# Indirect scatters and gathers issued one at a time in a fused attention and mixture-of-experts layer

## The reference

```python
x = x + _layernorm(attn(_layernorm(x)))          # 16 heads, exp decay on the scores
# feed-forward part, flat = _layernorm(x) as 4096 x 256
out = einsum('tnm,nmd->td', silu(gs) * us, wd_s)             # 2 shared experts, 128 wide
probs = softmax(flat @ router_w)                             # 16 experts
weights, indices = top_k(probs, 2); weights /= weights.sum()
h = silu(g) * u * comb[:, :, None]                           # 16 routed experts, 64 wide
out = out + einsum('tem,emd->td', h, wd_r)
x = x + _layernorm(out)
```

## Time and profile before

| | us |
|---|---|
| three runs | 1548.79 to 1557.74, median 1553.58 |
| profiled execution | 1557.02 |
| its span | 1554.5 |
| attention and what is ahead of it | about the first 1119 |
| routing and blocks 0 to 3 of pairs, up to the first gather | 1119 to 1372 |
| pairs of the second sequence, with gathers of blocks 0 to 3 | 1372 to 1484 |
| gathers of blocks 4 to 7 and the end | 1484 to 1554 |

### The profile page before, as it was taken

The page is one execution under the profiler, slowest core; times in us unless marked ns, Lnnn a source line. Parts: engine busy times, 40 slices in busy tenths (PEclk is TensorE's granted clock), DMA queues, the critical chain, the costliest instruction groups (busy, mean ns, idle before and its releaser), DMA issues. The chain is left out here.

```text
span 1554.5 us, 27193 instructions
## 1 busy us (share of the span) xinstructions
PE 1342.6 (86%) x8496; PEld 603.5 (39%) x8497; DVE 553.2 (36%) x1704; ACT 1146.8 (74%) x1419; POOL 189.7 (12%) x239
## 2 busy tenths in 40 slices
PE   7759999999999999999999999999688766666681
PEld 4523333333333333333333333333356555545441
DVE  5603323233232232322313121122254754615634
ACT  4449999999999989999999999999544434313422
POOL 1000000000000000000000000000034522232363
PEclk9979999999999999999999999999888888888886
DMA  7575466555664557555665465459422433445532
GB/s 186 224 163 136 116 141 157 121 135 127 152 157 97 135 145 155 145 115 130 157 132 135 104 134 102 88 131 248 103 81 95 139 106 116 148 124 170 184 111 86
DMA packets 139538, 210.96 MB, mean 136 GB/s; under 512 B 56336, under 2 KB 102288, under 8 KB 130960
## 3 DMA queue, kind: packets, MB, share of 16 engines
q1 hardware_dynamic: 133328, 193.38, 50.3%
q0 software_dynamic: 6144, 16.79, 3.3%
HBM read 147.19 MB, written 67.11 MB: 138 GB/s over the span
## 5 line engine op out<-in xcount | busy, mean ns | idle before, releaser
L705 ACT ACTIVATE work<-ps 128x1024 f32<-128x1024 f32 x1024 | 951.4, 1084 | 71.9 <-DVE ps L541 38.0
L636 PE MATMUL ps<-work 128*32 128x512 f32 x4096 | 548.1, 607 | 0.0
L628 PE MATMUL ps<-Q_st,K_st 64*128 64x512 f32 (+3 forms) x2432 | 441.1, 430 | 44.6 <-ACT work L705 28.1
L628 PEld LDWEIGHTS ps<-Q_st,K_st 64*128 64x128 f32 x2432 | 231.3, 185 | 543.2 <-ACT work L705 452.0
L541 DVE TENSOR_TENSOR ps<-ps,small 128x128 f32<-128x128 f32 x512 | 153.3, 299 | 743.1 <-PE ps L628 741.5
L505 POOL COPY work<-V_all 128x256 f32 (+1 forms) x32 | 12.9, 403 | 924.3 <-PE ps L636 924.2
L636 PEld LDWEIGHTS ps<-work 128*32 128x32 f32 x4096 | 80.9, 108 | 114.0 <-issue 88.1
L2058 POOL DMA_INDIRECT xT<-y_dram,decay x64 | 64.1, 1002 | 60.8 <-DMA y_dram<-work 42.5
L2046 POOL DMA_INDIRECT xs_dram<-part,decay x64 | 64.0, 1000 | 47.5 <-issue 47.5
L2215 PE MATMUL ps<-stack,work 128*128 x384 | 61.0, 310 | 10.0 <-issue 9.8
L2197 PE MATMUL ps<-ident,work 128*128 128x128 f32 x192 | 35.9, 318 | 32.1 <-DVE work L2271 17.3
(11 more groups left out here) (181 smaller groups left out, 1035.8 us busy)
## 6 DMA issues: line engine op xcount, KB each, us to landing
K_st<-halves_dram SPq DMA_DIRECT2D x256, 256.0 KB, 5.6
halves_dram<-work SPq DMA_DIRECT2D x64, 512.0 KB, 3.7
Q_st<-halves_dram SPq DMA_DIRECT2D x256, 128.0 KB, 5.6
work<-xs_dram SPq DMA_DIRECT2D x96, 128.0 KB
y_dram<-work SPq DMA_DIRECT2D x48, 256.0 KB
work<-in_L_attn_x SPq DMA_DIRECT2D x16, 512.0 KB, 7.4
attn_dram<-work SPq DMA_DIRECT2D x16, 256.0 KB, 6.6
work<-attn_dram SPq DMA_DIRECT2D x8, 512.0 KB
```

Source lines behind the costliest of these rows:

```text
L628: m = nc.tensor.matmul(ps[:, half_of(s, half) + c % 2, q0 % CH:q0 % CH + w], K_st[tile, par, a, s * P:(s + 1) * P], Q_st[tile, par, a, at: ...
L636: m = nc.tensor.matmul(ps[STRIP * c:STRIP * (c + 1), ACC + par], Vg[:, par, s], probs[:, probs_of(par, s), chunk(c)], start=s == 0, stop=s ...
L705: nc.scalar.activation(probs[:, probs_of(par, s), half * HALF:(half + 1) * HALF], src, ACT.Exp, scale=SCALE).then_inc(s_["exp_done"], 1)
```

## The change

Three things are changed.

1. `few_calls` puts a wait ahead of each scatter, and ahead of each gather of blocks 0 to 3: it is issued when the one before it has landed. The gathers of blocks 4 to 7 get no such wait.
2. The places in `ORDER` move. The last four scatter calls of most blocks stand behind `S1` of the block after the next; `GA` becomes eight calls in four entries, and the additions `SM` of blocks 0 to 3 start at the slots 6, 10, 14 and 18, where they started at 5, 9, 13 and 16.
3. The loads of the attention result and of x for block 1 (`next_block`) are issued ahead of the store of the last pair of heads, inside the attention part.

```diff
@@ attention, SyncE
             first_block["weights"](sp, 1)
+            first_block["next_block"](sp)
             store_att(NPAIR - 1)
-            first_block["next_block"](sp)
@@ layer, ORDER
     for r in (1, 2):
         ORDER += [("T1", r + 1), ("LA", r + 2), ("D", r - 1, 0), ("Y", r + 1), ("Z", r - 1, 0), ("T2", r), ("D", r - 1, 1), ("S1", r + 1),
...
-        ORDER += [("SC", r, j) for j in range(CT)]
+                  ("SC", r - 1, 2), ("SC", r - 1, 3), ("LG", r), ("Z", r - 1, 1), ("N1", r + 1, 0), ("N1", r + 1, 1), ("LX", r + 2), ("U", r, 0), ("EX", r), ("U", r, 1), ("S2", r + 1),
+                  ("TP", r, 0), ("TP", r, 1), ("H", r, 0), ("RK", r), ("H", r, 1), ("N2", r + 1), ("PL", r), ("CA", r), ("SC", r, 0), ("SC", r, 1)]
...
-    behind[-1] += [("GA", 0), ("GA", 1)]
-    for n, i in enumerate((5, 9, 13, 16)):
+    behind[NP + 2] = []
+    for n, i in enumerate((6, 10, 14, 18)):
+        for j in range(CT):
+            behind[4 * n + j - 1].append(("GA", n, j))
         for k in range(4):
             behind[i + k].append(("SM", n, k))
         behind[i + 4] += [("ST", n, 0)]
         behind[i + 5] += [("ST", n, 1), ("F3", n)]
-        if n < 2:
-            behind[i + 5].append(("GA", n + 2))
@@ layer, GpSimd
+            def few_calls(done, k):
+                k -= 1
+                if k >= 0:
+                    n = k // (2 * CT)
+                    pool.wait_ge(done[n % 2], 16 * (2 * CT * (n // 2) + k % (2 * CT) + 1))
+
             def scatter(r, j):
...
                 for i in range(2):
+                    few_calls(put_done, 2 * CT * r + 2 * j + i)
                     at = put_at[:, r * CT + j, i:i + 1]
...
-            def gather(n):
+            def gather(n, j):
...
-                need(pool, sum_sb, 2 * (n - 1))
-                for j in range(CT):
-                    for i in range(2):
-                        at = get_at[:, n * CT + j, i:i + 1]
+                if j == 0:
+                    need(pool, sum_sb, 2 * (n - 1))
+                for i in range(2):
+                    if n < 4:
+                        few_calls(yg_in, 2 * CT * n + 2 * j + i)
+                    at = get_at[:, n * CT + j, i:i + 1]
```

More of the change, by code:

```diff
@@ L1572, in layer @@
         ORDER += [("P", 1, i)] + behind[i]
+    gathers = lambda n: [("GA", n, j) for j in range(CT)]
     sums = lambda n: [("SM", n, k) for k in range(4)]
@@ L1575, in layer @@
     norm = lambda n: [("N3", n, 0), ("N3", n, 1)]
-    ORDER += [("GA", 4), ("GA", 5), ("U", 5, 0), ("H", 5, 0), ("U", 5, 1), ("H", 5, 1), ("U", 6, 0), ("D", 5, 0), ("D", 5, 1), ("Z", 5, 0), ("Z", 5, 1), ("U", 6, 1)]
-    ORDER += sums(4) + [("H", 6, 0)] + stats(4) + [("F3", 4), ("GA", 6), ("U", 7, 0), ("H", 6, 1), ("D", 6, 0)] + norm(4) + [("D", 6, 1), ("Z", 6, 0), ("Z", 6, 1), ("U", 7, 1)]
-    ORDER += sums(5) + [("H", 7, 0), ("AD", 4)] + stats(5) + [("F3", 5), ("GA", 7), ("H", 7, 1), ("D", 7, 0), ("D", 7, 1)] + norm(5) + [("Z", 7, 0), ("Z", 7, 1)]
+    ORDER += gathers(4) + gathers(5) + [("U", 5, 0), ("H", 5, 0)] + behind[NP + 2] + [("U", 5, 1), ("H", 5, 1), ("U", 6, 0), ("D", 5, 0), ("D", 5, 1), ("Z", 5, 0), ("Z", 5, 1), ("U", 6, 1)]
+    ORDER += sums(4) + [("H", 6, 0)] + stats(4) + [("F3", 4)] + gathers(6) + [("U", 7, 0), ("H", 6, 1), ("D", 6, 0)] + norm(4) + [("D", 6, 1), ("Z", 6, 0), ("Z", 6, 1), ("U", 7, 1)]
+    ORDER += sums(5) + [("H", 7, 0), ("AD", 4)] + stats(5) + [("F3", 5)] + gathers(7) + [("H", 7, 1), ("D", 7, 0), ("D", 7, 1)] + norm(5) + [("Z", 7, 0), ("Z", 7, 1)]
     ORDER += sums(6) + [("AD", 5)] + stats(6) + [("F3", 6)] + norm(6)
@@ L2044, in scatter @@
                 for i in range(2):
+                    few_calls(put_done, 2 * CT * r + 2 * j + i)
                     at = put_at[:, r * CT + j, i:i + 1]
                     nc.gpsimd.indirect_dma_start(xs_dram[r // 4], bass.IndirectOffsetOnAxis(ap=at, axis=0), xn[r % 2][:, j], None).then_inc(put_done[r % 2], 16)
-            def gather(n):
+            def gather(n, j):
                 b = n // 4
-                if n % 4 == 0:
+                if n % 4 == 0 and j == 0:
                     pool.wait_ge(get_sb, b + 1)
@@ L2074, in _ @@
                 elif what == "GA":
-                    gather(n)
+                    gather(n, at[0])
                 elif what == "F3":
```

19 lines of the change are left out of this document (7 added, 12 removed).

## The result

The changed kernel takes 1579.2 us (median of four runs, 1579.1 to 1582.3). The kernel before, on the same chip, took 1555.7. The ratio is 1.0158, with an interval of 1.0112 to 1.0203: slower by some 24 us. The forecast was 1566, so the direction held and the time lies in the range, but half of the loss was not foreseen.

What follows compares the result with a forecast made beforehand. ScalarE's exps fill the unchanged attention part; in the last 440 us engines stall behind GpSimd's DMA trains. Routing +11 (start included), scatters -10, gathers +11.2: +12 on 1557.0, 1569, as median 1566 us; range 1535 to 1592.

Steps and rivals of the forecast that it cites:

- the standstills: After attention: VectorE and ScalarE idle with input ready while GpSimd's indirect calls run; some 54.5 us on the chain.
- remote: Profile's mark for idle time released by another core or an unknown queue; 11.0% of 495 us from 1060 on.
- the twelve: Twelve chain pieces of such idle time, 1241.10 to 1518, each said to end inside a train or within 2 us.
- the standstills stay: Rival: trains don't cause them, or single calls hold engines as long; scatters' -10 becomes 0, +22, 1576 us; chance 0.10.
- p: Time from one indirect call's start to the next's when waiting for landing; 3.0 us for scatters, 3.1 for gathers.
- a lone call lands sooner: Rival: a lone call lands sooner than a train's last, p = 2.5; sum -18, 1536 us; chance 0.27.
- Start: Block 1's transposes after attention: load issued some 10 us earlier, transposes at about 1120; -4.7 us, bounds 1.7 to 5.
- Routing: Blocks 0 to 3: waiting scatter calls delay GpSimd's small powers on the path; +11 us, the start's gain included.
- The walk: Routing, call by call: S2 of block 2 as before, then +1.8 and +8.2 us, second_norm +1.
- Scatters 4 to 7: Beside pairs: 17.2 us of standstill go, late fetches cost 3.5, some 3.5 left for short standstills; -10 us.
- Gathers: Blocks 0 to 3 beside the second sequence: 32 chained calls land 17.1 us later, 5.9 less follows; +11.2 us.
- Tail: Gathers of blocks 4 to 7 keep their trains, standstills and time; 0 us.

Runs made afterwards that it cites:

- e1: Changed kernel with the wait ahead of each scatter taken away, gathers of blocks 0 to 3 still waiting; ratio 1.0073 to the kernel before.
- e2: Changed kernel with the wait ahead of each gather taken away, scatters still waiting; ratio 1.0017 to the kernel before.
- e3: Changed kernel with both kinds of waits taken away, leaving the new order and the early loads; ratio 0.9900 to the kernel before.
- e10: e3 with four gather calls in flight for blocks 0 to 3; ratio 0.9888 to the kernel before.
- e11: e3 with each gathered row of blocks 0 to 3 cut from 1024 to 256 bytes; ratio 0.9891 to the kernel before.
- e14: e3 with GpSimd filling four single columns behind each gather call of blocks 0 to 3; ratio 0.9880 to the kernel before.
- e4: Kernel before with only the loads of block 1 moved ahead of attention's last store; ratio 0.9994 to the kernel before.
- e13: Changed kernel's order with two calls in flight for all scatters and all gathers; ratio 0.9838 to the kernel before.
- e8: e3 with the scatters of blocks 4 to 7 chained, all other calls free; ratio 0.9829 to the kernel before.
- e9: e3 with two gather calls in flight for blocks 0 to 3; ratio 0.9787 to the kernel before.
- e15: e3 with GpSimd filling 256 columns and waiting for that fill behind each gather call of blocks 0 to 3; 1514.5 us, ratio 0.9751 to the kernel before.
- e12: e9 with the scatters of blocks 4 to 7 chained as in e8; 1518.4 us, ratio 0.9754 to the kernel before.

## Why the prediction was right, and where not

**Right.** The direction and its main reason. A wait for each landing costs more than the standstills that it removes: shown by the two-by-two of e1, e2, e3 and after. The standstills belong to the trains: "remote" is gone from the chain of the changed kernel, and comes back in the gather stage with calls at full rate (e3, e10, e11, e14), though not every train has them (see the tail below). They end inside a train or behind it as forecast; but two of the twelve end 2.2 and 3.0 us after the last call (1517.97 against 1515.76, 1394.61 against 1391.64), not within 2. The rival "the standstills stay" is out. p for scatters was taken as 3.0 and is 2.67 alone and 2.97 over scatter 2; the 2.5 of the rival "a lone call lands sooner" was reached by no two neighbouring calls.

**Start, -4.7 forecast.** The transposes of block 1 began 2.1 us earlier, still waiting for the load, where the earlier trace rows has 6.86 us of idle time:

```profile
1122.81 1.94 PE L1646 MATMUL ps<-ident,work 128*128 128x128 f32 x8 [4.68 <-DMA work<-attn_dram]
```

That is just above the lower bound (1.7). The load was issued 10.8 us earlier, at 1108.41, but landed only 14 us later; it stands behind the weights, and the forecast had put it there by 1120. e4, with this edit alone, shows no difference in time.

**Routing, +11 forecast, +20.2 measured: the term that was mis-sized first.** The walk was right in kind, as GpSimd's timeline shows:

```profile
1164.95 0.96 POOL L2051 DMA_INDIRECT xs_dram<-part,decay  x1 [1.71 <-DMA xs_dram<-part,decay]
1165.93 1.04 POOL L1723 TENSOR_TENSOR small<-small 128x4 f32<-128x4 f32 x1
...
1192.85 1.04 POOL L1723 TENSOR_TENSOR small<-small 128x4 f32<-128x4 f32 x1
...
1222.70 1.14 POOL L2051 DMA_INDIRECT xs_dram<-part,decay  x1 [2.50 <-DMA xs_dram<-part,decay]
1227.55 1.55 POOL L2051 DMA_INDIRECT xs_dram<-part,decay  x1 [3.70 <-DMA xs_dram<-part,decay]
1230.81 0.96 POOL L2051 DMA_INDIRECT xs_dram<-part,decay  x1 [1.71 <-DMA xs_dram<-part,decay]
1231.79 1.04 POOL L1723 TENSOR_TENSOR small<-small 128x4 f32<-128x4 f32 x1
```

`S2` stands right behind a call each time, with no idle time of its own. Against the earlier trace rows, `S2` of block 2 came 2.8 us later (forecast 0), the step to block 3 took 26.9 us (forecast 21.8 + 1.8), and the step to block 4 took 38.9 (27.9 + 8.2). The missing 9.2 us are three terms, 8.7 us, and small change:

- The start: scatter 0 began at 1142.94, not at 1140.9, and `S1` of block 2 came 1.7 us later than the walk has it.
- Four calls ahead of `S2`, put at 10.0 us: 11.0, 10.7 and 12.7, together 4.4 us too little. The 22 distances within the groups of calls have a mean of 3.12, so the 3.0 was nearly right as a mean. But it was taken as a constant, and sixteen of the 22 are 2.66 to 3.01, the other six 3.3 to 4.9. The slow ones stood ahead of `S2`, while the two groups ahead of `S1` took 9.3 and 9.0 and gained nothing, as `S1` was not due yet.
- `second_norm` of block 2, put at 0.4 us a time: its factors were ready at 1167.25, but it waited until 1169.12 for the last call of scatter 0, which was 4.17 us on its way. With that `S1` of block 3 was due 15.0 us behind `S2` of block 2, not 12.4: 2.6 us.

What makes a call slow was not tested, but the trace has a pattern that the forecast didn't use. Up to 1232 all five calls that took over 3.5 us to land went out less than 2 us behind the issue of a 512 KB load by SyncE (1157.47, 1164.73, 1184.67, 1200.34, 1220.99); most others took 2.40. Two of the loads, and on the chain the two calls:

```profile
1157.47 0.37 SPq L1625 DMA_DIRECT2D work<-in_L_attn_x  x1
1184.67 0.37 SPq L1625 DMA_DIRECT2D work<-in_L_attn_x  x1
...
1157.80 4.21 DMA xs_dram<-part,decay
1185.00 3.93 DMA xs_dram<-part,decay
```

All of `second_norm`, on ScalarE, has 20.9 us of idle time put down to landed scatters, part of it beside other waits; the kernel before has none there:

```profile
L1703 ACT ACTIVATE part<-V_all,small 128x256 f32<-128x256 f32 x28 | 14.5, 588 | 39.5 <-DMA xs_dram<-part,decay 20.9
```

**Scatters 4 to 7, -10 forecast, -15.1 measured.** Of the 15.1, 8.3 come without any waiting for landings (143.1 before, 134.8 in e3): the new order, in which `S1` no longer stands behind eight calls, and the earlier loads (3.6 in e4, whose order is the old one). The prediction took the moves only as places where the waits fall and gave them no gain. The chain's own part is -6.8 by the changed kernel (134.8 to 128.0) and -2.8 by e2 (132.0), less than the -10 either way.

**Gathers, +11.2 forecast, +22.2 measured.** Two terms. From the first call to the last call of block 3 the distance was 3.36 us, (1481.19 - 1376.91) / 31, in place of 3.1: 104.3 - 96.1 = 8.2 us. One of the 31 is no landing: the call at 1457.41 waited for VectorE's additions and came 4.98 us after the one before. From there to the gathers of block 4 passed 29.8 us, of which 2.8 are the landing; 24.1 had been left for the remaining 27.0: 2.9 us. Together 11.1 of the missing 11.0. That `F3` stands behind the calls was read from the order and thought harmless; it is two of the four gaps. What failed here is again the size of p, and the reading that the two factors in its queue cost nothing.

**Tail, 0 forecast, -5.1 measured.** Its gathers wait for no landing in any kernel but e13. In before, e4, e8 and e10 the tail takes 71 us, and the chain there has "another core or an unknown queue" at 17.8 to 18.3%, 13 us; in after, e1, e3, e9, e11, e14 and e15 it takes 64 to 67 and the chain has none. So the same train stands still in one kernel and not in another, and where it does the tail is mostly 5 us longer (in e2 it is not: 66.8 us with 17.4%; e12 lies between, 68.0 us with 8.4%). The -5.1 is taken for this and not for the change; what decides it was not found.

**The cause behind the standstills** was "taken" in the prediction: that the engines' own next instructions arrive by a queue that the train holds up. Nothing here shows it. In e3 the gaps end at 1377.02 and 1382.61, and between 1368 and 1390 the trace has no packet of an instruction queue at all. ScalarE and VectorE often come back together (1382.70 and 1382.61) while each waits for a result of TensorE that is already done, as far as the profile, which models the ends of matmuls, can say. And the bytes don't matter. What is shown is a condition for the gather stage: standstills at 1.25 to 1.30 us a call, next to none at 1.55. What it holds up stays open.

## What to carry to other kernels

- When a train of software-issued DMAs disturbs other engines, first try a slightly slower train: 0.3 us more per call gave 20 us here, one call at a time lost 27 in the same place. Count all that stands behind a wait on its queue, small operations of another stage above all.
- Price a serial chain by the mean distance of its calls, outliers included, and ask which of its calls can be slow: a slow one right ahead of an operation on the path costs in full, a fast one ahead of an operation that isn't due gains nothing.
- Reordering and waiting that come in one change have to be timed apart: here they were -15 and +40 us.

## What the runs showed of the hardware that was not expected

- Lone indirect calls of 128 rows of 1 KB on GpSimd, each waiting for the one before: the next starts 2.67 us (scatter) or 2.93 us and more (gather, beside fetches) after the start of the one before. Scatter calls issued less than 2 us behind a 512 KB load of SyncE took 3.9 to 4.6 us to land, most others 2.40.
- Trains of such calls at 1.25 to 1.30 us can leave ScalarE and VectorE idle for 4 to 14 us at a time, "remote", with TensorE's result ready; at 1.55 us between calls, or with two in flight, they hardly do. Rows of 256 bytes do it like rows of 1024. Not every such train does it: none ahead of 1233 in the kernel before, and in the last blocks only those of some kernels.
- Single columns filled by GpSimd (four in 0.20 us) disappear in the 0.30 us that it leaves between two calls anyhow.
